# Row fetches addressed in bytes, nine a group on SyncE and ten on ScalarE, in a graph attention kernel

## What is computed

```python
w_ij = silu(edge_feats @ rad_W1 + rad_b1) @ rad_W2 + rad_b2
w_ij = w_ij + (silu(chi_scalar @ sph_W1 + sph_b1) @ sph_W2 + sph_b2)
q_i = (x @ Wq)[receivers];  k_j = (x @ Wk)[senders];  v_j = (x @ Wv)[senders]     # 8 heads of 16
alpha = (q_i * w_ij * k_j).sum(axis=-1) / sqrt(16) * cutoffs[:, None]             # one per edge and head
out = segment_sum(alpha[..., None] * v_j, receivers) / 16
return layernorm(x + out)
```

## Time and profile before

| | |
|---|---|
| device time, 3 runs | 2024.70, 2027.39, 2027.53 us; median 2027.39 |
| the profiled execution | 2026.94 us, its span 2025.6 us |
| TensorE, VectorE, ScalarE, POOL busy | 85%, 74%, 28%, 74% of the span |
| granted TensorE clock, mean | 0.927 |
| indirect DMAs of the main loop on POOL | 1542 |
| row DMAs | 2688 on SP, 3200 on ACT |

### The profile page before, as it was taken

One profiled execution on the slowest core, in us unless ns is written; L12 is line 12 of the kernel. 1 busy time (PEld: TensorE's weight loads), 2 busy tenths in 40 slices (PEclk: granted clock), 3 DMA queues, 4 the chain that ended last, 5 costly groups with the idle time before them and its releaser, 6 DMA issues. The chain is left out here.

```text
span 2025.6 us, 59667 instructions
## 1 busy us (share of the span) xinstructions
PE 1714.1 (85%) x14497; PEld 1249.1 (62%) x14497; DVE 1493.6 (74%) x3816; ACT 561.4 (28%) x955; POOL 1490.6 (74%) x1575
## 2 busy tenths in 40 slices
PE   7699888889888888888888888888988888888885
PEld 6466666666666666666666665566656656566664
DVE  4388878888777777777777776777777777777775
ACT  4333223322222222222222222222222222222223
POOL 6757777777777777777777777777777777777771
PEclk9799999999989998999898888989998988998897
DMA  9856666666666656565565656656565565665643
GB/s 328 264 146 166 161 168 171 170 170 171 170 171 169 162 158 161 159 169 160 161 168 152 169 156 165 167 152 170 151 169 161 158 170 150 170 164 156 169 120 95
DMA packets 194097, 338.54 MB, mean 167 GB/s; under 512 B 81093, under 2 KB 107061, under 8 KB 193749
## 3 DMA queue, kind: packets, MB, share of 16 engines
q0 software_dynamic: 74784, 203.79, 36.9%
q1 hardware_dynamic: 111832, 126.33, 21.9%
q10 hardware_dynamic: 7132, 4.59, 1.0%
HBM read 319.59 MB, written 14.95 MB: 165 GB/s over the span
## 5 line engine op out<-in xcount | busy, mean ns | idle before, releaser
L518 POOL DMA_INDIRECT kvt<-kvtab,srcS x1542 | 1463.6, 949 | 488.4 <-issue 470.9
L592 ACT ACTIVATE hs<-bank,B 128x512 f32<-128x512 f32 x806 | 510.2, 684 | 1388.3 <-PE bank L530 993.4
L686 DVE TENSOR_TENSOR t<-bank,kvt 128x512 f32<-128x512 f32 (+1 forms) x397 | 268.5, 676 | 402.1 <-DMA kvt<-kvtab,srcS 210.2
L553 PE MATMUL bank<-W2r,hs 128*128 128x128 f32 x3224 | 508.6, 305 | 2.7 <-ACT hs L592 2.7
L553 PEld LDWEIGHTS bank<-W2r,hs 128*128 128x128 f32 x3224 | 427.3, 206 | 93.1 <-issue 81.7
L553 PE MATMUL bank<-W2s,hs 128*128 128x128 f32 x3224 | 459.8, 289 | 0.0
L553 PEld LDWEIGHTS bank<-W2s,hs 128*128 128x128 f32 x3224 | 427.4, 206 | 0.0
L563 PE MATMUL bank<-msg,oh 128*32 128x128 f32 x3224 | 181.8, 297 | 248.1 <-DVE accT L640 240.0
L563 PEld LDWEIGHTS bank<-msg,oh 128*32 128x32 f32 x3224 | 72.2, 111 | 442.5 <-issue 441.8
L696 DVE TENSOR_REDUCE bank<-t 128x32 f32<-128x512 f32 x403 | 280.1, 695 | 13.9
L694 DVE TENSOR_TENSOR t<-bank,t 128x512 f32<-128x512 f32 x403 | 273.6, 679 | 12.5 <-PE bank L543 12.4
(11 more groups left out here) (79 smaller groups left out, 491.8 us busy)
## 6 DMA issues: line engine op xcount, KB each, us to landing
eft<-in_ef SPq DMA_DIRECT2D x101, 512.0 KB
kvA<-kvtab ACTq DMA_DIRECT2D x3200, 1.0 KB
kvS<-kvtab SPq DMA_DIRECT2D x2688, 1.0 KB
dbt<-dst SPq DMA_DIRECT2D x101, 384.0 KB
kvt<-kvtab,srcS POOLq DMA_INDIRECT x1542
qwt<-qtab SPq DMA_DIRECT2D x403, 24.0 KB
kvtab<-kvt SPq DMA_DIRECT2D x24, 256.0 KB, 6.9
qtab<-qx SPq DMA_DIRECT2D x12, 384.0 KB, 6.5
```

Source lines behind the costliest of these rows:

```text
L518: pool.indirect_dma_start(kvt[:, (g - HX) % KS, t, :], None, kvtab, bass.IndirectOffsetOnAxis(ap=srcS[:, g * TG + t:g * TG + t + 1], axis= ...
L553: pe.matmul(WB[g % 2][:, t * D:(t + 1) * D], hs[:, g % HS, j, t * 128:(t + 1) * 128], w2[:, :], start=(j == 0 and t == 0), stop=False, ski ...
L592: act.activation(hs[:, g % HS, j, :], HB[i % 4][:, :], ACT.Silu, bias=B1[:, j:j + 1]).then_inc(m_si, 1)
L686: m = dve.tensor_tensor(t1[:, s, a:b, :], tiles(WB[s][:, :])[:, a:b, :], kv[:, :, 0:D], ALU.mult)
```

## The change

A row's place in the table becomes an offset in bytes that stands ready in the register. The host's tables still hold node numbers; VectorE multiplies `rowsS` and `rowsA` by 1024 once, in the prologue, and makes `baseq`, the windows' starts times 768. The DMAs then take a byte view of the tables (`kv_bytes`, `q_bytes`) at the register itself, with no `snap` and no multiplication. RS goes from 7 to 9, RA from 8 to 10. The registers are loaded every two groups, 20 at a time (LS and LA: 18 and 20, rounded up to fours), where it was every four groups, 28 and 32 at a time.

```diff
-RS, RA = 7, 8
+RS, RA = 9, 10
+LS, LA = -(-2 * RS // 4) * 4, -(-2 * RA // 4) * 4
...
+    u8 = mybir.dt.uint8
+    KVROW, QROW = 4 * 2 * D, 2 * NPART * D
+    kv_bytes = kvtab.rearrange("n f -> (n f)").bitcast(u8)
+    q_bytes = qtab.rearrange("n f -> (n f)").bitcast(u8)
...
-        rowsS = sb("rowsS", [NG // 4, 4 * RS], i32)
-        rowsA = sb("rowsA", [NG // 4, 4 * RA], i32)
+        rowsS = sb("rowsS", [NG // 4, 2 * LS], i32)
+        rowsA = sb("rowsA", [NG // 4, 2 * LA], i32)
...
             dve.tensor_copy(basei[:, :], base[0:1, :]).then_inc(s_win, 1)
+            dve.tensor_scalar(baseq[:, :], base[0:1, :], float(QROW), None, ALU.mult).then_inc(s_win, 1)
...
+                    dve.wait_ge(s_rows, 32)
+                    for rows in (rowsS, rowsA):
+                        dve.tensor_scalar(rows[:, :], rows[:, :], float(KVROW), None, ALU.mult).then_inc(s_bytes, 1)
...
+            def start_of(reg, last):
+                return bass.RuntimeValue.of_register_unchecked(reg, min_val=0, max_val=last)
+
+            def kv_row(reg):
+                return kv_bytes[bass.ds(start_of(reg, (N - 1) * KVROW), KVROW)].rearrange("(o f) -> o f", o=1)
...
             def sp_rows(g):
-                if g % 4 == 0:
-                    sp.load(sp_row, rowsS[g // 4:g // 4 + 1, :])
+                if g % 2 == 0:
+                    sp.load(sp_row, rowsS[g // 4:g // 4 + 1, g % 4 // 2 * LS:(g % 4 // 2 + 1) * LS])
                 for r in range(RS * g, RS * (g + 1)):
...
-                        row = sp.snap(sp_row[r % (4 * RS)], min_val=0, max_val=N - 1)
-                        sp.dma_start(kvS[p:p + 1, u % 2, :], kvtab[bass.ds(row, 1), :]).then_inc(m_kvS[u % 2], 16)
+                        sp.dma_start(kvS[p:p + 1, u % 2, :].bitcast(u8), kv_row(sp_row[r % (2 * RS)])
+                                     ).then_inc(m_kvS[u % 2], 16)
```

More of the change, by code:

```diff
@@ L104, in gnn_program @@
         basei = sb("basei", [1, NG], i32)
+        baseq = sb("baseq", [1, NG], i32)
         npass = sb("npass", [1, 1], i32)
@@ L165, in gnn_program @@
                                         "par", "dbi", "cut", "src", "src2")]
-            s_rows = sem("s_rows")
+            s_rows, s_bytes = sem("s_rows"), sem("s_bytes")
             s_xp, s_xc, s_hp, s_ha, s_hd = [sem(f"s_{n}") for n in ("xp", "xc", "hp", "ha", "hd")]
@@ L403, in gnn_program @@
                 nqo[b % QN] += 16
-            dve.wait_ge(s_win, 4)
+            dve.wait_ge(s_win, 5)
             for eng in (act, dve):
@@ L410, in gnn_program @@
                     eng.wait_ge(s_qo[i], nqo[i])
-            act.wait_ge(s_win, 4)
+            act.wait_ge(s_win, 5)
             act.wait_ge(s_q3, NQB)
@@ L415, in gnn_program @@
                     eng.wait_ge(s_kvo[i], nkv[i])
-            sp.wait_ge(s_rows, 32)
-            act.wait_ge(s_rows, 32)
+            sp.wait_ge(s_bytes, 2)
+            act.wait_ge(s_bytes, 2)
             dve.wait_ge(s_ha, HX)
@@ L422, in gnn_program @@
             pe.wait_ge(s_xc, HX)
-            sp.wait_ge(s_win, 4)
+            sp.wait_ge(s_win, 5)
             pe.wait_ge(s_w1, 4)
@@ L455, in gnn_program @@
         dve_base = [dve.alloc_register(f"dve_base{i}") for i in range(4)]
-        sp_row = [sp.alloc_register(f"sp_row{i}") for i in range(4 * RS)]
-        act_row = [act.alloc_register(f"act_row{i}") for i in range(4 * RA)]
+        sp_row = [sp.alloc_register(f"sp_row{i}") for i in range(LS)]
+        act_row = [act.alloc_register(f"act_row{i}") for i in range(LA)]
         with nc.Fori(0, passes):
-            def window_start(eng, regs, g):
-                if g % 4 == 0:
-                    eng.load(regs, basei[0:1, g:g + 4])
-                return eng.snap(regs[g % 4], min_val=0, max_val=NQ - W)
+            def start_of(reg, last):
+                return bass.RuntimeValue.of_register_unchecked(reg, min_val=0, max_val=last)
+            def kv_row(reg):
+                return kv_bytes[bass.ds(start_of(reg, (N - 1) * KVROW), KVROW)].rearrange("(o f) -> o f", o=1)
             def features(q):
@@ L505, in gnn_program @@
                     sp.wait_ge(m_q, g - QS + 1)
-                at = window_start(sp, sp_base, g)
-                sp.dma_start(qwt[:, g % QS, :],
-                             qtab[bass.ds(at, W), :].rearrange("n (c f) -> (n c) f", c=NPART)
+                if g % 4 == 0:
+                    sp.load(sp_base, baseq[0:1, g:g + 4])
+                at = start_of(sp_base[g % 4], (NQ - W) * QROW)
+                sp.dma_start(qwt[:, g % QS, :].bitcast(u8),
+                             q_bytes[bass.ds(at, W * QROW)].rearrange("(n f) -> n f", n=W * NPART)
                              ).then_inc(m_qw[g % QS], 16)
@@ L598, in act_rows @@
             def act_rows(g):
-                if g % 4 == 0:
-                    act.load(act_row, rowsA[g // 4:g // 4 + 1, :])
+                if g % 2 == 0:
+                    act.load(act_row, rowsA[g // 4:g // 4 + 1, g % 4 // 2 * LA:(g % 4 // 2 + 1) * LA])
                 for r in range(act_rows_upto(g), act_rows_upto(g + 1)):
@@ L605, in act_rows @@
                             act.wait_ge(m_msg, at_a[u - 2] + 1)
-                        row = act.snap(act_row[r % (4 * RA)], min_val=0, max_val=N - 1)
-                        act.dma_start(kvA[p:p + 1, u % 2, :], kvtab[bass.ds(row, 1), :]).then_inc(m_kvA[u % 2], 16)
+                        act.dma_start(kvA[p:p + 1, u % 2, :].bitcast(u8), kv_row(act_row[r % (2 * RA)])
+                                      ).then_inc(m_kvA[u % 2], 16)
             for g in range(NE):
@@ L635, in accumulate @@
             def accumulate(g):
-                at = window_start(dve, dve_base, g)
+                if g % 4 == 0:
+                    dve.load(dve_base, basei[0:1, g:g + 4])
+                at = dve.snap(dve_base[g % 4], min_val=0, max_val=NQ - W)
                 dve.wait_ge(m_fold, g + 1)
@@ L721, in gnn_program @@
             dve.tensor_copy(basei[:, :], base[0:1, :]).then_inc(m_up, 1)
+            dve.tensor_scalar(baseq[:, :], base[0:1, :], float(QROW), None, ALU.mult).then_inc(m_up, 1)
             dve.wait_ge(m_acc, NE)
-            dve.wait_ge(m_up, 4)
+            dve.wait_ge(m_up, 5)
             for i in range(KS):
@@ L867, in row_table @@
         flat[:128 * len(at)] = src_tiles[at, TG - 1].reshape(-1)
-        return flat.reshape(ng // 4, 4 * rate)
+        pairs = flat.reshape(ng // 2, 2 * rate)
+        return np.pad(pairs, ((0, 0), (0, -2 * rate % 4))).reshape(ng // 4, -1)
     at_s, at_a = row_plan(-(-n_edges // G))
```

## The result

The change makes the kernel slower: 2078.01 us median (2073.01 to 2079.95, 4 runs) against 2027.46 us (2024.70 to 2030.40, 4 runs), ratio 1.024 with a 95% interval of 1.022 to 1.026. I had forecast 2012.7 us and a range up to 2024, so the sign is wrong too. The profiled execution took 2078.51 us, its span is 2077.2 us and its mean granted TensorE clock 0.929, against 0.927 before; the clock has no part in it.

The account below looks back on a forecast made before the run. POOL's gathers were taken to set the end. 15.0 us gained less 0.3 at the start is 14.7, taking the profiled 2026.94 to 2012.2; with 0.45 for the median, 2012.7 us, range 2009.5 to 2024.

Parts of the forecast that it names:

- What bounds the kernel before: Main loop: POOL's unbroken row of gathers, 1.2537 us each, sets the end at 4.87 us a group.
- POOL, 12 gathers fewer, 15.0 us: POOL's gathers: 13 fewer, one only lengthening its early wait; 12 at 1.2537 us each gain 15.0 us.
- SP, a row and a load: SP's fetches: a row 0.336 us after 0.419, a load of 20 registers 1.30 us, a group 4.59 us.
- The rival that takes SP's own issue for the bound: Row fetches and loads of `sp_rows`: SP decides from 4.70 us a group; chance 0.05 for part of the gain, 0.09 slower.
- One engine for the rows: DMA queues: if all rows lay on one engine, its load goes from 0.87 to 0.96 and still fits, closely.
- The rival built on it: One DMA engine fills up if rows cost it a fifth more: 2090 us; chance 0.05, shared with exclusion of issues.
- 8 us behind SP's last window: End of the kernel: VectorE's last sum comes some 8 us behind SP's last window where SP sets the pace.
- ACT at the start, prologue, end: ACT in the first groups costs 0.3 us, bounds 0 and 1.5; prologue nothing, at most 1 us; end nothing.
- The rival of exclusion: DMA issues of SP and ACT exclude one another: 4.95 us a group, about 2110; chance 0.05, shared with a full engine.
- The signs of being wrong: SP's queue never waits and POOL waits long for VectorE, or DMA instructions of rows get longer than 0.24 us.

Follow-up runs that it names:

- e1: Changed kernel with the old rates, 7 rows a group on SP and 8 on ACT: 2026.00 us, ratio 1.0001 to the kernel before.
- e10: Changed kernel with 8 rows a group on SP and 9 on ACT, 17 in all: 2014.95 us, ratio 0.9957 to the kernel before.
- e9: Changed kernel with 9 rows a group on SP and 9 on ACT, 18 in all: 2015.37 us, ratio 0.9953 to the kernel before.
- e2: Changed kernel with 9 rows a group on SP and 6 on ACT, 15 in all: 2024.71 us, ratio 0.9999 to the kernel before.
- Run 12: Changed kernel whose row transfers bring 64 bytes instead of 1024 from each buffer's third use on: 2076.88 us, ratio 1.026 to the kernel before.
- e11: Changed kernel, 9 and 10 rows, in which POOL gathers nothing from group 100 on: 1953.06 us, ratio 0.9646 to the kernel before.
- run 15: Changed kernel with each row cut in two pieces of 512 bytes, 9 rows a group on SP and 1 on ACT: 3147.18 us.
- e13: Changed kernel, 9 and 10 rows, with the old address arithmetic at each row fetch: 2266.77 us, ratio 1.1166 to the kernel before.

## Why the prediction was wrong

**What bounds the kernel before: right.** e1, with the change's addressing and the old rates, keeps the time of before to 0.1%, and e10 gets faster with fewer gathers.

**POOL, 12 gathers fewer, 15.0 us: right in kind.** e9 leaves out ten (1532 against 1542) and e10 seven (1535), with gains of 8.7 and 9.1 us, where 1.25 each would give 12.5 and 8.8. With the full 13 it could not be collected.

**SP, a row and a load: right.** 0.323 measured against 0.336, a load of 20 1.40 against 1.30 and on ACT 1.46 against 1.56, a group 4.47 where nothing interferes (e2) against 4.59. The rival that takes SP's own issue for the bound had its place right, the rows of `sp_rows`, and its cause wrong.

**"One engine for the rows": this is the step that failed.** It took the share of time that packets have in ACT's queue, 1.0% of sixteen engines, spread it over all rows, added 0.58 for the rest, and got 0.96 of an engine: "the work would still fit, closely". The rival built on it got 2090 us, near the 2078 that came, and shared a chance of 0.05 with another. Both terms were of the wrong kind. Run 12 halves the packets' time and the pace stays. The right measure is rows in a time, over stretches in which the resource is full and the gathers run at POOL's pace, 1.25 us apart:

| kernel | rows a group | us a group | us a row |
|---|---|---|---|
| e1, 160 to 310 us | 15 | 3.98 | 0.265 |
| e10, 200 to 500 us | 17 | 4.57 | 0.269 |
| e9 | 18 | 4.72 | 0.262 |
| changed kernel | 19 | 4.89 | 0.257 |
| e12, rows of 64 bytes | 19 | 4.90 | 0.258 |

A row needs 0.26 us beside the gathers, whoever issues it; e11 has it at 4.52/19 = 0.238 or less without them. The change wants 19 rows in POOL's 4.83 us, 0.254 each, and that is just too little. Eighteen in 4.84 are 0.269, which is enough. The kernel before had 15 in 4.87. Even its SP-bound stretch, 15 in 4.35 or 0.290, stayed clear; and this row could have warned me, as the rate after was to be a seventh higher than anything the trace had shown.

That the resource is one DMA engine is the reading that the packets bear out: a whole row has one data packet, and those of SP and ACT are served one at a time. The sum of both queues counts (e1, e2, e9), and the gathers take part (e11). That their part is one share of each is argued from the few increments that come late; no row names an engine.

The Trainium skill, DMA: Bandwidth & Descriptors, section "Why a DMA increments its semaphore by 16 and not by 1", says that the number of engines, 16 at most, goes by the slowest dimension longer than one, that a tile of 128 partitions gets 16, that software can split a [1, N] transfer so that it goes out over several, that each engine which takes part writes the semaphore once, and that transfers of SP and ACT take the lowest-numbered. It has no example of such a row left whole, and the prediction gave the rule without its "longer than one". The trace settles it: one packet of 4 bytes for a whole row, two and sixteen for a cut one.

**How the loss adds up.** SP's windows end at 2019.7 in place of 1960.5, 59.2 us later. VectorE's last sum comes 25.2 us behind SP's last window, and came 32.0 behind it before, when SP ran ahead; 59.2 - 6.8 = 52.4 us is the shift of the last sum, 51.6 that of the profiled execution. I had put 8 us behind SP's last window. It is 25, and the 17 to 18 us until the last part of a window lands are most of it.

**ACT at the start, prologue, end:** no run singles them out. SP's first window goes out at 77.0, 2.1 us sooner than before, and my 0.3 us of loss can't be seen beside that.

**The rival of exclusion** was not it: e9 has nearly as many issues and loses nothing, and whole rows show no competition in their median. It has some truth in cut rows (0.07 us for a row of SP, 0.27 for a window, run 15). The Trainium skill, Perfetto Trace Analysis, section "DMA Instruction — HWDGE (DVE, Sync)", has the generator locked for one sequencer's use. The cut rows agree with such a lock; with whole rows no run shows it.

**The signs of being wrong** that the prediction named both came: SP's queue hardly waits while POOL waits 50 times for VectorE, and row instructions get longer than 0.24 us, up to 1.77.

## What to carry to other kernels

Many small DMAs from several queues can be bound by one shared DMA engine, with a price for each transfer (here the same for 64 and 1024 bytes): count transfers in a microsecond (here 3.8 beside the gathers, 0.26 us each), and don't read the packets' share of time, which says nothing is full. The sign in a profile is an issuing engine with no semaphore waits whose DMA instructions keep their median and grow a long maximum; then take one row off before taking the change back, since the edge is sharp (19 rows 2078, 18 rows 2015). An edit that makes issue cheaper and one that raises the rates are to be judged apart: the byte addresses were worth nothing at the old rates (e1) and 36 us at 8 and 9 rows, and the last row a group cost about 60.

## What the runs showed of the hardware that was not expected

- A row transfer of 64 bytes costs the shared resource as much as one of 1024 (4.90 against 4.89 us a group).
- The line before that resource is deep: rows start 13 us after SP's instruction has ended, which is 13/4.89 x 9 = 24 of SP's rows later, and with such a line the row's instruction itself takes up to 1.77 us. Where the line is short it takes 0.28 (before), 0.40 (e2) or 0.55 (e13) at most.
- A row in two pieces takes the issuing engine 0.56 to 0.64 us, one in sixteen pieces 0.54, a whole one 0.228.
- A packet of a whole row takes 46 ns in the median (a tenth of ACT's take over 0.30 us), and yet a row costs the engine 0.26 us beside the gathers. Where the rest of that time goes, no run here tells.
- One chip ran the kernel before in 3088 us, 1.52 times the 2024 to 2028 of three others, with 900 us of VectorE's waits put down to "remote". What that is was not tried; without gathers the time there fell to 2213.
